# Reordering the first three and the last three attention units on four engines, with the gate functions at the head of ScalarE's program

## What is computed

```python
def ref(x, ctx, g_xattn, g_ffn, ...):
    ln_out = _ln(_layernorm(x), ln_w, ln_b)
    q  = _ln(_fp8_linear(ln_out, wq))        # 16 heads of 128, 8 groups
    k  = _ln(_fp8_linear(ln_out, wk))
    v  = _fp8_linear(ln_out, wv)
    core = _gqa(q, k, v)
    qx = _ln(_fp8_linear(ln_out, wqx))
    kx, vx = split(ctx @ w_kv_x.T)
    xout = _gqa(qx, _ln(kx), vx)
    cat = quantise(concat(core, xout) / proj_smooth)
    x = x + tanh(g_xattn) * (cat @ wproj.T) * scale
    h = _layernorm(x)
    logits = 30 * tanh(h @ w_gate / 30)      # 8 experts, top 2 of them
    weights = softmax(logits) * top2_mask
    for e in range(8):
        out += silu(h @ w1[e]) * (h @ w3[e]) @ w2[e] * weights[:, e]
    return x + tanh(g_ffn) * out
```

## Time and profile before

| | us |
|---|---|
| median of 3 runs | 690.77 (689.95 to 691.3) |
| the profiled execution, its time | 690.51 |
| its span, first to last instruction | 688.6 |
| PE busy in the span | 641.4 (93%) |
| DVE busy | 602.5 (87%) |
| ACT busy | 550.8 (80%) |
| POOL busy | 464.6 (67%) |

### The profile page before, as it was taken

One profiled execution on the slowest core, in us unless ns is written; L12 is line 12 of the kernel. 1 busy time (PEld: TensorE's weight loads), 2 busy tenths in 40 slices (PEclk: granted clock), 3 DMA queues, 4 the chain that ended last, 5 costly groups with the idle time before them and its releaser, 6 DMA issues. The chain is left out here.

```text
span 688.6 us, 14974 instructions
## 1 busy us (share of the span) xinstructions
PE 641.4 (93%) x4573; PEld 588.6 (85%) x4574; DVE 602.5 (87%) x1386; ACT 550.8 (80%) x1927; POOL 464.6 (67%) x646
## 2 busy tenths in 40 slices
PE   1779999999999999999999999999998589999995
PEld 0778999999999999999999999999987578888884
DVE  6998899999989999998999999888899888777772
ACT  5898889989988999999899899988885356665671
POOL 4667687687777768867786787688664525565642
PEclk9999999999999999999999999999999789999999
DMA  7202000020020002102010110010079512233222
GB/s 227 62 0 87 7 1 31 3 62 32 1 62 1 32 1 63 32 1 62 1 32 2 56 32 12 29 35 1 1 294 399 171 39 41 54 50 53 50 41 27
DMA packets 35509, 37.72 MB, mean 55 GB/s; under 512 B 2704, under 2 KB 30352, under 8 KB 35440
## 3 DMA queue, kind: packets, MB, share of 16 engines
q1 hardware_dynamic: 31024, 30.84, 13.3%
q0 software_dynamic: 4416, 6.03, 5.2%
HBM read 31.62 MB, written 5.24 MB: 54 GB/s over the span
## 5 line engine op out<-in xcount | busy, mean ns | idle before, releaser
L1518 POOL TENSOR_SCALAR shared<-shared,rsum 128x256 f32<-128x256 f32 x256 | 142.3, 567 | 53.7 <-DVE rsum L1034 48.6
L717 ACT ACTIVATE shared<-s,nmax 128x256 f32<-128x256 f32 x256 | 122.4, 499 | 21.4 <-DVE nmax L1029 20.4
L1512 POOL TENSOR_TENSOR rstd<-rstd,half 128x7 f32<-128x7 f32 (+1 forms) x64 | 87.7, 1370 | 5.3
L1029 DVE TENSOR_REDUCE nmax<-s 128x2 f32<-128x512 f32 x128 | 86.9, 680 | 2.8 <-PE s L380 2.6
L1039 DVE TENSOR_TENSOR pt_lo<-t,pt_hi 128x512 fp32r<-128x512 f32 x124 | 84.2, 679 | 1.9 <-ACT pt_hi L725 0.9
L725 ACT CAST pt_hi<-t 128x512 fp32r<-128x512 f32 x124 | 74.1, 598 | 9.6 <-PE t L395 7.1
L733 ACT ACTIVATE shared<-route_bank,head_w 128x512 f32<-128x512 f32 (+1 forms) x124 | 81.6, 690 | 0.0
L336 PE MATMUL pj_a<-w_ring,xq 128*128 128x256 f32 x488 | 72.1, 291 | 7.9 <-POOL xq L1594 7.9
L380 PE MATMUL s<-qk_hi 128*128 128x256 f32 x256 | 77.5, 303 | 2.0 <-DVE qk_lo L1024 1.9
L1024 DVE TENSOR_TENSOR qk_lo<-shared,qk_hi 128x512 fp32r<-128x512 f32 x96 | 78.4, 816 | 1.1
L2072 DVE TENSOR_TENSOR w_lo<-expert_w,w_hi 128x1024 fp32r<-128x1024 f32 x46 | 56.3, 1225 | 23.7 <-ACT w_hi L1964 23.3
(11 more groups left out here) (281 smaller groups left out, 1951.8 us busy)
## 6 DMA issues: line engine op xcount, KB each, us to landing
expert_w<-in_w SPq DMA_DIRECT2D x24, 512.0 KB, 9.0
spare<-in_wT SPq DMA_DIRECT2D x19, 256.0 KB, 3.0
wp_raw<-in_wpT SPq DMA_DIRECT2D x16, 256.0 KB, 2.9
spare<-in_wkvT SPq DMA_DIRECT2D x16, 128.0 KB, 3.1
spare<-in_wT SPq DMA_DIRECT2D x9, 128.0 KB, 3.2
spare<-in_x SPq DMA_DIRECT2D x1, 1024.0 KB, 5.9
x_hat<-acc SPq DMA_DIRECT2D x1, 1024.0 KB, 4.6
out<-spare SPq DMA_DIRECT2D x1, 1024.0 KB, 8.5
```

The source lines that it names most:

```text
L717: e = act.activation(probs[:, st, h * S:(h + 1) * S], s_bank[st][:, h * S:(h + 1) * S], ACT.Exp, bias=nmax[:, st, h:h + 1], accum_out=psum ...
L1029: dve.tensor_reduce(nmax[:, st, :], s_bank[st][:].rearrange("p (h t) -> p h t", h=2), AX, ALU.max, negate=True).then_inc(max_done, 1)
L1512: pool.tensor_tensor(rstd[:, st, c], rstd[:, st, c], half[:, c], ALU.pow).then_inc(rstd_ready, 1)
L1518: m = pool.tensor_scalar(probs[:, st, c], probs[:, st, c], rsum[:, st, h:h + 1], 1.0, ALU.mult, ALU.mult)
```

## The change

No instruction is added or taken away but for a few repeated waits. The order of calls is another one in three places: the head of ACT's program, where both `tanh` come first; the hand-written part of the first three units on PE, ACT, DVE and POOL; and the hand-written part of the last three units with the routing, on the same four. The loop of units 1 to 28, the experts and SP's program stay as they are. The core of the diff, in this order: PE first units, PE last units, ACT head, DVE input stage, DVE routing, POOL head.

```diff
             pe.wait_ge(normq_done, 1)
             stay_awake(pj_a, 11)
-            turn_input(2)
             turn_heads(0, 0, 0, s_bank[0])
             turn_heads(0, 0, 1, s_bank[1])
+            turn_input(2)
             project_q(1, 0, 1, 1, pj_a, 1)
             turn_heads(0, 0, 2, pj_b)
 
             scores(0, 0, 0, 0)
             scores(0, 0, 0, 1)
-            pe.wait_ge(aff_done, 3)
-            project_kv(1, 0, 1, 1, pj_b, 1)
             pe.wait_ge(xq_y, 20)
             pe.wait_ge(v0_ready, 1)
             project_v0(pt_bank, 0)
             pe.wait_ge(normq_done, 3)
             stay_awake(o_bank, 5)
+            pe.wait_ge(aff_done, 3)
+            project_kv(1, 0, 1, 1, pj_b, 1)
             scores(0, 0, 1, 0)
             scores(0, 0, 1, 1)
+            stay_awake(o_bank, 4)
             pe.wait_ge(v0_split, 1)
             turn_probs(0, 0, 0)
-            stay_awake(o_bank, 4)
...
             steps(step)
             scores(29, 1, 0, 0)
             turn_probs(28, 1, 0)
-            out_project(G - 2, 0, 3, 27, 1)
-            scores(29, 1, 0, 1)
+            project_q(31, 1, 3, 0)
             turn_heads(30, 2, 0)
             turn_probs(28, 1, 1)
-            project_q(31, 1, 3, 0)
             project_kv(31, 1, 3, 0)
+            turn_heads(30, 2, 1)
+            scores(29, 1, 0, 1)
+            values(28, 0, 1)
+            turn_probs(29, 0, 0)
             scores(29, 1, 1, 0)
-            turn_probs(29, 0, 0)
-            values(28, 0, 1)
-            turn_heads(30, 2, 1)
             scores(29, 1, 1, 1)
+            out_project(G - 2, 0, 3, 27, 1)
+            turn_probs(29, 0, 1)
             project_q(31, 1, 3, 1)
...
+            act.wait_ge(cols_loaded, 32)
+            act.activation(gate[:, 0:1], col[:, C_SCAL + S_GX:C_SCAL + S_GX + 1], ACT.Tanh).then_inc(gated, 1)
+            act.activation(route.fgate[:], col[:, C_SCAL + S_GF:C_SCAL + S_GF + 1], ACT.Tanh).then_inc(route.f_gated, 1)
             act.wait_ge(consts_ready, 1)
             affine_in(0)
             affine_in(1)
@@ -800,68 +803,65 @@
             affine_in(3)
             affine_in(4)
             affine_in(5)
-            row_scale(1)
             affine_in(6)
             affine_in(7)
+            row_scale(1)
             affine_in(8)
-            act.wait_ge(cols_loaded, 32)
-            act.activation(gate[:, 0:1], col[:, C_SCAL + S_GX:C_SCAL + S_GX + 1], ACT.Tanh).then_inc(gated, 1)
-            affine_in(9)
-            act.activation(route.fgate[:], col[:, C_SCAL + S_GF:C_SCAL + S_GF + 1], ACT.Tanh).then_inc(route.f_gated, 1)
-            affine_in(10)
             weights_hi(0, 0, 2)
             weights_hi(0, 0, 3)
+            weights_hi(0, 0, 0)
             split_ctx(0)
+            weights_hi(0, 0, 1)
+            affine_in(9)
+            affine_in(10)
+            split_ctx(1)
...
             m.then_inc(w_scales_ready, 1)
             clip_in(0)
             round_in(0)
+            sum_weights(0, 1)
             clip_in(1)
-            sum_weights(0, 1)
+            sum_weights(0, 0)
+            round_in(1)
             clip_in(2)
-            round_in(1)
-            sum_weights(0, 0)
-            clip_in(3)
-            round_in(2)
             dve.wait_ge(w_scales_ready, 1)
             centre_weights(0, 0, (0, 1, 2, 3) + later_blocks(0))
             dve.wait_ge(v0_loaded, 16)
             dve.tensor_tensor(v0_raw, v0_raw, w_scale[:, :, 7:8].broadcast_to([P, KT, D]), ALU.mult).then_inc(v0_scaled, 1)
+            round_in(2)
             weights_lo(0, 0, 2)
             weights_lo(0, 0, 3)
             ctx_rest(0)
             weights_lo(0, 0, 0)
             weights_lo(0, 0, 1)
+            clip_in(3)
             round_in(3)
             row_stats(2)
...
             x1_begin()
             find_top(0)
-            choose(0)
+            x1_normalise(2)
             x1_tiles(3)
             x1_tiles(4)
             x1_normalise(3)
+            choose(0)
             x1_normalise(4)
+            find_top(1)
             first_places()
-            find_top(1)
             choose(1)
+            find_top(2)
+            choose(2)
             dve.wait_ge(chosen_ready, 2)
             with nc.allow_low_precision(reason="sums of up to six zeros and ones are exact"):
                 dve.tensor_reduce(chosen_sum[:], route.chosen[:, 0:NT - ST].rearrange("p t e -> p e t"), AX, ALU.add).then_inc(chosen_summed, 1)
-            find_top(2)
-            choose(2)
...
@@ -1597,8 +1597,8 @@
             pool.wait_ge(ones_set, 1)
             row_power(0)
             row_power(1)
+            row_shift(1)
             widen_in(0)
-            row_shift(1)
             centre_first()
```

219 lines of the change are left out of this document (107 added, 112 removed).

## The result

The changed kernel takes 685.02 us (median of four runs, 684.81 to 686.10) beside 691.02 us of the kernel before: a ratio of 0.9920, 95% interval 0.9909 to 0.9932. That is 6.0 us less, where the prediction had 3.0 (687.8, range 685.6 to 690.4): faster, as forecast, but by twice as much. A second series (e4_again, five rounds) gave 686.09 beside 691.50 (0.9918, 0.9904 to 0.9931), 5.4 us less.

A forecast was written before the change was run, and what follows sets the result against it. The loop of units 1 to 28 was taken as bound by TensorE's own work, leaving the ends: 690.51 - 2.0 (head) - 0.9 (tail) = 687.6 us, stated as 687.8 because the profiled execution was 0.26 below the median; range 685.6 to 690.4.

The forecast's parts named there:

- Head, step 1: ScalarE's start: the table load leaves the path, so the first affine_in starts at 7.7 instead of 9.07, 1.4 us earlier.
- Head, step 2: First weights on VectorE and POOL: centring starts earlier, and the last low part ends at about 19.7 instead of 21.17.
- Head, steps 3 and 4: First projection at 20.9 instead of 22.13, second weights issued at 19.7, unit 0's scores at 38.3 instead of 40.12.
- Head, step 5: Unit 0's scores to the loop: unit 1's first scores at 59.5 instead of 61.48, 2.0 us for the head.
- My upper bound of 3.0 for the head: Head gains no more than 3.0 us: 1.4 from the table load, 0.4 of v0, about 1.2 of waits.
- the rival of the gaining tail: Rival, end of kernel: the tail gains 3.0 us, giving 685.8 us; chance 0.09.
- Step 1: Tail's start: scores(29, 1, 0, 1) goes about 3 us later; TensorE loses about 1.2 us at the next pair of scores.
- step 2: Tail, 511 to 527 us: the 1.2 us are made good in TensorE's waits; values(31, 0) comes at the same time.
- Step 3: Tail, 527 to 536 us: last values end 0.2 us earlier, unit 31's out-projection starts about 0.9 earlier.
- Step 4: Tail's routing: x1_normalise(2) goes behind find_top(0); last ranking at 545.9 instead of 546.76, 0.9 us earlier.
- The clock takes the head's gain: Rival, head: TensorE idles about 2 us ahead of the heads, its clock falls, 0.5 us is left; 689.4; chance 0.17.
- The tail gains 3: Rival, tail: it gains 3.0 us beside the head's 2.0, for 685.8 us; chance 0.09.

The follow-up runs named there:

- e4_again: The changed kernel unaltered, timed again beside the kernel before: 686.09 us beside 691.50, ratio 0.9918.
- e3: The kernel before with only the two tanh moved first on ScalarE: 690.13 us beside 691.50.
- e9: The kernel before with both tanh first and the new input-stage order on ScalarE, VectorE and POOL, all else old: 688.48 us beside 692.09.
- e1: The kernel before with every changed line ahead of the loop, on all four engines, and none behind it: 687.07 us beside 691.50.
- e13_low_later: The kernel of e3 with POOL's wp_lo(0, 0, 0) moved behind heads_hi(0, 0, 0): 690.66 us beside 690.87 of the kernel before.
- e5_turn: The kernel of e3 with TensorE's turn_input(2) moved behind unit 0's first two turn_heads: 691.24 us beside 691.52 of the kernel before.
- e2_tail: The kernel before with every changed line behind the loop and none ahead of it: 690.23 us, 1.3 us less, ratio 0.9970 to 0.9995.
- e7: The kernel before with only the routing's order: rank(0) on TensorE and VectorE's lines from x1_begin: 691.41 us beside 691.52.
- e11: The kernel before with the rest of e2_tail, the new order of the last three units without e7's routing lines: 691.85 us beside 692.09.
- e15: The kernel of e11 with VectorE's x1_normalise(2) moved behind find_top(0): 689.42 us beside 690.87 of the kernel before.
- e14_turn_both: The kernel of e5_turn with ScalarE's affine_in(16) also moved, behind affine(0, 1): 689.59 us beside 690.87 of the kernel before.

## Why the prediction was too cautious

The direction and the way the gain is carried were right, and the tail's size nearly so. The term that failed is the head's: 2.0 us forecast, 4.1 measured. It failed in two places: step 2 put the end of the low parts 0.9 us too late, and steps 3 and 4 took POOL's `wp_lo` as costing nothing, where its collision with VectorE is worth 0.97 us. What the profiled executions show, each as the start in us and how much earlier than before:

| place | before | forecast | tanh alone (e3) | with input order (e9) | all (after) |
|---|---|---|---|---|---|
| first projection | 22.13 | 20.9 (1.2) | 20.62 (1.5) | 20.52 (1.6) | 20.04 (2.1) |
| second weights summed | 27.13 | 25.6 (1.5) | 25.40 (1.7) | 24.74 (2.4) | 24.52 (2.6) |
| unit 0's scores | 40.12 | 38.3 (1.8) | 38.44 (1.7) | 37.34 (2.8) | 36.56 (3.6) |
| mark | 61.48 | 59.5 (2.0) | 59.80 (1.7) | 58.56 (2.9) | 57.38 (4.1) |

**Head, step 1** (1.4 us by the table load) was right: 9.07 - 7.81 = 1.3 at `affine_in`, 1.4 in time by e3_gates.

**Head, step 2** put the end of the low parts at 19.7; they ended at 18.76. I had kept's durations, 3.10 us for VectorE's centring among them, and centring took 1.93 here, while v0's product took 0.84 instead of 0.41 and one pair of low parts 1.69 instead of 1.28. The three together are 4.46 us instead of 4.79. From the start of centring to the end of the low parts I had 6.9 us and it was 6.31 (6.44 before): 0.33 of that is these durations, 0.1 the rounding, which took 0.2 and not 0.3, and the rest what I had left in case ScalarE was late, which it wasn't. The start was 0.35 earlier than forecast. Which of the three was long differs between executions: in e1 and e4, with the same head, centring took 2.78 us and the other two 0.42 and 1.28 to 1.29, and the stretch was 6.33 us in both.

**Head, steps 3 and 4.** Everything that hangs on the low parts came about 0.9 us earlier than forecast: the second weights were issued at 18.78, not 19.7, the first projection started at 20.04, not 20.9. Behind them I missed one term altogether: `wp_lo` stands in the diff, two lines apart from where it was, and I costed it at nothing. The four products and `wp_lo`, in the kernel before and then in the changed one:

```profile
32.66 2.08 DVE L1115 TENSOR_SCALAR spare<-spare,w_mean,w_scale 128x128 f32<-128x128 f32 x4
33.30 1.35 POOL L1559 TENSOR_TENSOR wp_ring<-wp_raw,wp_ring 128x512 fp32r<-128x512 f32 x1
```

```profile
27.69 1.28 POOL L1559 TENSOR_TENSOR wp_ring<-wp_raw,wp_ring 128x512 fp32r<-128x512 f32 x1
...
30.20 1.11 DVE L1115 TENSOR_SCALAR spare<-spare,w_mean,w_scale 128x128 f32<-128x128 f32 x4
```

Before, it held VectorE's products of the second weights for about 1 us (2.08 us for four of them at 32.66, 1.11 after), in the row that sets unit 0's heads; e13_low_later shows 0.95 us for it. It goes away in e9_input too, where `wp_lo` stands in its old place and only comes later than the products; so the order alone does not decide it, the moment does. v0's 0.4 us out of the row was right. From the sums of the second weights to the heads the row is 7.44 us instead of 8.26.

**Head, step 5** gave 0.2 us to the orders behind unit 0's scores; it is 21.36 - 20.82 = 0.5. What I said of `turn_input(2)` was incomplete: its move frees nothing alone. In e5_turn the mark came 1.8 us later than in e3_gates; by the estimate above up to about 1.2 us of that are a low clock.

So the head's 4.10 us are 2.61 up to the sums of the second weights (forecast 1.5), 0.82 in the row from there to the heads (about 0.3), 0.13 from the heads to the scores and 0.54 from there to the mark (0.2 together). Of the 2.1 us beyond the forecast, 1.1 thus stand ahead of the sums, 0.5 in that row and 0.5 behind the heads; for the last part I have no single cause. In the row of 0.82 the collision gave 0.97 and v0 0.33, and a later start of centring and of `normalise_q` took 0.5 back. My upper bound of 3.0 for the head counted waits only and held every duration fixed, and no rival had a head better than 2.0: the range ended at 685.6, just below the rival of the gaining tail.

**Tail.** 0.9 us forecast; 1.08 in the profiles whose clock held and 1.3 in time (e2_tail). Step 1 (a new wait ahead of `scores(29, 1, 1, 1)`) is there: 0.66 us at 494.05 in the changed kernel. It was made good, as step 2 said: from the loop's end to the last `values` it is 52.46 us instead of 52.74. Step 3 (out-projection 0.9 earlier) is 0.86. Step 4 was right as a whole, and e7, e11 and e15 show that steps 3 and 4 are one: step 3's 0.86 us is lost again to a wait of 1.80 us unless `find_top(0)` goes ahead of `x1_normalise(2)`.

**The rivals.** "The clock takes the head's gain" fell for the changed kernel: 1.00 from 20 to 80 us after, where TensorE idled 0.75 us ahead of the heads and not the 2 us of the rival, and in the kernel before the dip of the earlier trace rows cost nothing up to the mark (21.36 us from the scores, 21.39 in e2_tail without it). With the 2 us the rival came true: e5_turn and e14_turn_both, as shown there. In the changed kernel a low clock did take a gain, but the tail's, in some executions: about 1.0 us (13.85 against 12.82). "The tail gains 3" gave nearly the measured time for the wrong reason.

**The loop** carried the difference: 4.10 us at the mark, 4.46 at its end (3.94 and 4.19 in e1_head, 3.61 and 3.65 in e4_again). What it seems to add lies within the spread of all profiles from the mark to the loop's end, 0.7 us.

**What stays open:** why POOL is held in one execution and VectorE in another; what decides whether the clock falls 4.3 or over 8 us behind the last `values`, and whether it is low for a while at 525 to 530; what the middle's order is worth alone; and what the two moves of e14_turn_both are worth at full clock.

## What to carry to other kernels

A reorder's gain is bounded by waits plus the durations that change with what stands beside them: before costing a moved instruction of POOL at nothing, look at which of VectorE's instructions it ran beside and which it will. A wait that moves on one engine has partners on the others: list, for the moved call, every instruction that waits for it and what is queued behind each: one right line (`find_top` ahead of `x1_normalise`) was worth all that a dozen others had prepared. Look at the idle time, too, that a moved call leaves where it stood: behind 2.0 us of it TensorE's clock was low in the profiles of e5 and e14. (Idle time alone does not decide it: 1.90 us ahead of unit 0's scores were followed by a low clock in the kernel before, 1.91 in e2_tail were not.) And where the clock can fall within the stretch that is read, one profile isn't enough: the same tail read as 0.05 and 1.08 us.
